# Three parts of expert tiles instead of two halves, results gathered at the join

## The chip, the cores and the metric

The kernel runs on one core of a Trainium2 chip. The metric is the device time of one execution in microseconds. The engines are TensorE (PE in the profile, PEld for its weight loads), VectorE (DVE), ScalarE (ACT), GpSimd (POOL) and SyncE (SP), which here only issues transfers.

## What is computed

One transformer layer on 2048 tokens of 128 features: attention with 16 heads and an ALiBi causal mask, then a mixture of 8 experts of which each token uses 2.

```python
h = _layernorm(x, axis=-1) * (1 + ca) + sa
x = x + ga * _L0_attn_ref(h, ...)                 # 16 heads of 8, causal, ALiBi
h = _layernorm(x, axis=-1) * (1 + cb) + sb
x = x + gb * _L0_ffn_ref(h, ...)
# _L0_ffn_ref:
logits = xf @ router_w.T
probs = jax.nn.softmax(logits, axis=-1)
top_w, top_idx = jax.lax.top_k(probs, TOPK)       # TOPK = 2
top_w = jax.nn.softmax(top_w, axis=-1)
h = jax.nn.silu(jnp.einsum('td,efd->tef', xf, w1))   # E = 8, F = 512
y = jnp.einsum('tef,edf->ted', h, w2) * expert_scale[None, :, None]
out = jnp.einsum("te,ted->td", combine, y)        # combine: the two weights of each token, else 0
```

## The kernel before, in words

Tokens lie in 16 blocks of 128, and four blocks make a chunk. Attention runs in four groups of four heads; a group has 36 steps over keys and queries (`STEPS`). In a step TensorE computes scores (L738), ScalarE exponentiates them (L1210) and TensorE multiplies by the values (L705). VectorE finds row maxima for the next group meanwhile (L966); in the last group it has none left from about step 17 on, and does other work beside the steps: the norm of each chunk's sums (L923 to L932), the residual after the projection (L608, L990), statistics, the scaled tokens (L866), and, after the transposes (L562) and the router's product (L625), the routing (`route`, L1007 to L1041).

Experts are worked on in tiles of 128 rows that belong to one expert. `count` (L633, L636) counts on TensorE how many tokens each expert gets, `place` (L1051 to L1064) turns that into a row of `slot_scratch` in DRAM for each token and choice, and an expert for each tile. This is done once for each half of the tokens, 8 blocks; a half has 16 + 7 = 23 tiles, so that every expert's rows fit. GpSimd's `send` (L1369) scatters a half's tokens, 2 x 8 indirect transfers of 128 rows. Each row also carries its weight and the row to which its result goes.

A tile then takes: SP loads the expert's w1 and the 128 rows (L517, L522); TensorE transposes the rows (L803); ScalarE scales them (L1231); TensorE multiplies by w1 (`up`, L812), ScalarE applies silu (L1237), TensorE multiplies by w2 (`down`, L822); VectorE copies w2 into place three tiles ahead (L1084) and multiplies the result by weight and gate (`keep`, L1092); GpSimd scatters it to its place in `y_scratch` (L1418). TensorE runs `up(j)` ahead of `down(j - 1)`. Every engine's program is a fixed order written out by hand; engines meet at semaphores. The first half's places are made at step 29 of the last group, the scatter follows; the second half's are made at tile 9, and GpSimd then stands its 16 scatters ahead of the results of tiles 9 and later. Between the last attention step and tile 0 come the norm, projection, residual, statistics and transposes of the last chunk. When a half's results are in DRAM, SP reads them back in order of the tokens (L530), VectorE adds them (L1098, L1099), and SP stores the output (L534).

Of the kernel before, what the change touches and what calls it, by code (L numbers as in the profile page):

```python
# [149 lines left out]
TABLES_AT, EMPTY_AT, BLANK_AT = 5, [6, 7, 8, 9], [11, 20, 25]  # L150
BIAS_AT = [28, 30, 32, 34]
NORM_AT = {12: 0, 17: 1, 21: 2}
PROJECT = {18: 0, 19: 1, 23: 2}
RESIDUAL = {18: 0, 19: 1, 24: 2}
TOKENS = {20: 0, 21: 1, 28: 2}
DOUBLE = {22: 0, 23: 1, 28: 2}
TURN = {21: 0, 22: 1, 28: 2}
LOGITS = {23: [0, 1], 30: [2]}
KEEP_LOGITS = {23: [0, 1], 30: [2]}
ROUTE = {23: 0, 24: 1, 25: 2, 26: 3, 27: 4, 28: 5}  # L160
ROUTE_EXP = {23: 0, 26: 1}
COUNT_AT = 26
PLACE_AT = 29


HALFN = NT // 2
ROW = C + 2
NTILE = HALFN * TOPK + E - 1
TILES = 2 * NTILE
DEEP = 4  # L170
FAR = 14


LATE_ROUTE = {1: 0, 3: 1, 4: 2, 5: 3, 6: 4, 8: 5}
LATE_EXP = {2: 0, 7: 1}
LATE_COUNT, LATE_PLACE = 7, 9
JOIN_AT = {NTILE + 8: 0, NTILE + 10: 1}
# [29 lines left out]
def build(nc, a):  # L207
# [3 lines left out]
    with ExitStack() as ctx:  # L211
# [90 lines left out]

        slots = sb("slots", [P, NT, TOPK, ROW])
        slots_u = slots.bitcast(mybir.dt.uint32)
# [4 lines left out]
        count_to = sb("count_to", [P, NTILE])  # L309
        more = sb("more", [P, E, E])  # L310
        tiles_of = sb("tiles_of", [P, 2, E])
        tiles_to = sb("tiles_to", [P, 2, E])
        base_at = sb("base_at", [P, E])
        passed = sb("passed", [P, NTILE, E])
        owner = sb("owner", [P, NTILE])
        expert = sb("expert", [P, 2, NTILE], mybir.dt.int32)
        spot = sb("spot", [P, 2, HALFN, E])
        spot_f = sb("spot_f", [P, 2, HALFN])
        spots = sb("spots", [P, TOPK, NT], mybir.dt.uint32)
        xt = sb("xt", [P, FAR, ROW])  # L320
        xt_u = xt.bitcast(mybir.dt.uint32)
# [5 lines left out]
        yfin = old1[:, 0:2 * TPC * TOPK * C].rearrange("p (a n k c) -> p a n k c", a=2, n=TPC, k=TOPK)  # L327
        yt = old1[:, 2 * TPC * TOPK * C:(2 * TPC * TOPK + FAR) * C].rearrange("p (k c) -> p k c", c=C)
# [8 lines left out]
        slot_dram = nc.dram_tensor("slot_scratch", (TILES * P, ROW), fp32, kind="Internal").ap()  # L337
        y_dram = nc.dram_tensor("y_scratch", (TOPK * T + TILES * P, C), fp32, kind="Internal").ap()
# [26 lines left out]
        tables_s, blank_s, blank_out = sem("tables_s"), sem("blank_s"), sem("blank_out")  # L365
        both_s, count_ps, place_s, sent_in = sem("both_s"), sem("count_ps"), sem("place_s"), sem("sent_in")
        xt_in, w1s_in = [sem(f"xt_in{k}") for k in range(FAR)], [sem(f"w1s_in{k}") for k in range(DEEP)]
        w2s_s, tT_ps, tT_s, up_ps, silu_s, down_ps, yt_s = (sem(n) for n in ("w2s_s", "tT_ps", "tT_s", "up_ps", "silu_s", "down_ps", "yt_s"))
        y_out = [sem(f"y_out{k}") for k in range(FAR)]
        y_in = [sem("y_in0"), sem("y_in1")]  # L370
# [44 lines left out]
        def tile_outs(j):  # L415

            return [(k, 16 * len(range(k, j, FAR))) for k in range(FAR) if j > k]
# [8 lines left out]
        def _(sp):  # L426
# [30 lines left out]
            def group(g, first, last):  # L457
                for p in range(-1, NSTEP):
# [10 lines left out]
                    if g == 1 and p in BLANK_AT[:2]:  # L469
                        k = BLANK_AT.index(p)  # L470
                        sp.wait_ge(blank_s, k + 1)
                        q0, q1 = (0, NT * TOPK) if k == 0 else (NT * TOPK, TILES)
                        dst = slot_dram.rearrange("(p q) c -> p (q c)", q=TILES)[:, q0 * ROW:q1 * ROW]
                        sp.dma_start(dst, slots[:, :, :, :].rearrange("p n k c -> p (n k c)")[:, 0:(q1 - q0) * ROW]).then_inc(blank_out, 16)
# [34 lines left out]
            def load_tile(j):  # L509

                k, x, half = j % DEEP, j % FAR, j // NTILE
                if j % NTILE == 0:
                    sp.wait_ge(place_s, half + 1)
                e = sp.value_load(expert[0:1, half, j % NTILE:j % NTILE + 1], min_val=0, max_val=E - 1)
                if j >= DEEP:
                    sp.wait_ge(up_ps, j - DEEP + 1)
                sp.dma_start(w1s[:, k, :], a["w1T"][:, ds(e * F, F)]).then_inc(w1s_in[k], 16)  # L517
                if j % NTILE == 0:
                    sp.wait_ge(sent_in, 16 * TOPK * HALFN * (half + 1))
                if j >= FAR:  # L520
                    sp.wait_ge(y_out[x], 16 * (j // FAR))
                sp.dma_start(xt[:, x, :], slot_dram[j * P:(j + 1) * P, :]).then_inc(xt_in[x], 16)  # L522

            def load_results(c):
                for k, n in tile_outs(NTILE * (c // 2 + 1)):
                    sp.wait_ge(y_out[k], n)
                src = y_dram[c * CW * TOPK:(c + 1) * CW * TOPK, :].rearrange("(n p k) c -> p n k c", p=P, k=TOPK)
                if c >= 2:
                    sp.wait_ge(joined, c - 1)
                sp.dma_start(yfin[:, c % 2, :, :, :], src).then_inc(y_in[c % 2], 16)  # L530

            def store_output(c):
                sp.wait_ge(joined, c + 1)
                sp.dma_start(o_v[:, c * TPC:(c + 1) * TPC, :], x_sb[:, c * TPC:(c + 1) * TPC, :]).then_inc(stored, 16)  # L534
# [311 lines left out]
        def _(dve):  # L846
# [273 lines left out]
            for c in range(2, NC_):  # L1120
                join(c)
# [354 lines left out]
```

## Time and profile before

| | |
|---|---|
| median of 3 runs | 635.05 us (630.54 to 641.14) |
| the profiled execution | 638.27 us |
| its span, first to last instruction | 636.4 us |
| TensorE busy | 506.6 us (80%) |
| VectorE busy | 442.6 us (70%) |
| ScalarE busy | 396.3 us (62%) |
| GpSimd busy | 154.8 us (24%) |
| mean granted clock of TensorE | 0.892 |

The busy shares are means over the whole span. A row of a timeline gives start, duration, engine, line, operation, tiles and count, and in brackets the idle time before it and what ended it. All times are microseconds from the start of the span. "Issue" is time in which an engine waited for nothing that the profile shows, "remote" a release by something that it doesn't show. Ends of matrix products are modelled.

### The profile page before, as it was taken

Reading aid. Unit: us, or ns where it says so; the run is one execution under the profiler, and the core shown is the slowest. Engines: PE = TensorE matmul, PEld = TensorE weight load, DVE = VectorE, ACT = ScalarE, POOL = GpSimd, SP = SyncE. Lnnn points to the kernel's source line nnn. Section 1 sums busy time; section 2 is a strip of 40 time slices with the busy share of each in tenths; the row PEclk is TensorE's granted clock in tenths of the full one; section 3 lists DMA queues with packets and bytes.
Section 4 is the critical chain, followed back from the end, with each engine's and each line's share of the span. In section 5 each row is a group of like instructions: output and inputs, shape, how many; then the busy total and the mean of one; then the engine's idle time right before and its main releaser. Section 6 shows DMA issues by size and latency. Waiting matters only on the chain.

```text
span 636.4 us, 14860 instructions
## 1 busy us (share of the span) xinstructions
PE 506.6 (80%) x5756; PEld 266.6 (42%) x5756; DVE 442.6 (70%) x677; ACT 396.3 (62%) x760; POOL 154.8 (24%) x250
## 2 busy tenths in 40 slices
PE   4657788899998999979999997979644886279991
PEld 2422232333433432423432432434212886279891
DVE  3789989899989989869989899586303264024532
ACT  4822456688887888768888887765622562035450
POOL 3410000001041114103031103051540135734451
PEclk9955899999999999979999999996857689569997
DMA  5691600000154013241000001000120244246863
GB/s 143 210 283 23 102 2 1 3 4 5 34 87 155 3 62 133 51 66 20 2 4 2 3 9 19 3 1 1 51 80 21 72 145 143 75 123 202 255 203 115
DMA packets 36627, 46.33 MB, mean 73 GB/s; under 512 B 6328, under 2 KB 27512, under 8 KB 36184
## 3 DMA queue, kind: packets, MB, share of 16 engines
q1 hardware_dynamic: 33728, 39.84, 23.5%
q0 software_dynamic: 2496, 5.15, 2.3%
q8 instruction: 46, 0.75, 0.5%
q10 hardware_dynamic: 336, 0.42, 0.2%
q14 instruction: 21, 0.17, 0.1%
HBM read 29.45 MB, written 15.74 MB: 71 GB/s over the span
## 4 chain that ended last, share of the span: by engine, by line
PE 44%; DVE 7%; issue 6%; ACT 6%; DMA 4%; another core or an unknown queue 2%; SPq 1%; POOL 1%; DVEq 0%; POOLq 0%; ACTq 0%
PE pv L705 14%; PE b L738 9%; PE b L812 6%; PE b L822 5%; ACT probs L1210 5%; PE b L677 4%; DVE part L966 2%; PE b L652 2%; DMA xt<-slot_scratch 1%; DMA y_scratch<-aug,xt 1%; DVE slots L866 1%; DMA sums_scratch<-raw 1%; ACT raw L1182 1%; PE b L803 1%
## 5 line engine op out<-in xcount | busy, mean ns | idle before, releaser
L1210 ACT ACTIVATE probs<-b 128x512 f32<-128x512 f32 (+1 forms) x576 | 298.6, 570 | 106.5 <-PE b L652 38.2
L966 DVE TENSOR_REDUCE part<-b 128x2 f32<-128x1024 f32 (+2 forms) x320 | 327.1, 1060 | 32.8 <-PE b L677 15.7
L705 PE MATMUL pv<-probs,v_cur 128*32 128x256 f32 (+1 forms) x2432 | 181.5, 380 | 2.8 <-issue 2.5
L738 PE MATMUL b<-aug 55*128 55x512 bf16 (+3 forms) x640 | 116.8, 362 | 37.4 <-ACT probs L1210 28.7
L677 PE MATMUL b<-aug 52*128 52x512 bf16 (+3 forms) x640 | 118.0, 369 | 22.3 <-DVE part L966 19.9
L738 PEld LDWEIGHTS b<-aug 55*128 55x128 bf16 x640 | 36.8, 94 | 154.2 <-ACT probs L1210 139.6
L705 PEld LDWEIGHTS pv<-probs,v_cur 128*32 128x32 f32 x2432 | 50.7, 110 | 72.4 <-issue 43.7
L812 PE MATMUL b<-hTt,aug 128*128 128x128 f32 x368 | 54.1, 295 | 11.0 <-issue 10.2
L822 PE MATMUL b<-aug,hst 128*128 128x128 f32 x368 | 53.0, 292 | 11.9 <-issue 9.9
L1092 DVE SCALAR_TENSOR_TENSOR aug<-b,xt,gate 128x128 f32<-128x128 f32 x46 | 16.1, 350 | 64.0 <-PE b L822 31.9
L1418 POOL DMA_INDIRECT y_scratch<-aug,xt x46 | 44.6, 970 | 63.0 <-DVE aug L1092 60.9
L812 PEld LDWEIGHTS b<-hTt,aug 128*128 128x128 f32 x368 | 49.9, 210 | 12.0 <-issue 12.0
L822 PEld LDWEIGHTS b<-aug,hst 128*128 128x128 f32 x368 | 49.0, 207 | 12.6 <-issue 11.7
L677 PEld LDWEIGHTS b<-aug 52*128 52x128 bf16 x640 | 34.0, 96 | 38.6 <-DVE part L966 31.5
L1237 ACT ACTIVATE hst<-b 128x512 f32<-128x512 f32 x46 | 27.5, 597 | 33.3 <-PE b L812 14.1
L1231 ACT ACTIVATE hTt<-b,modc 128x128 f32<-128x128 f32 x46 | 20.9, 456 | 36.4 <-PE b L803 23.7
L1326 POOL CAST nmp<-nmax 128x16 bf16<-128x16 f32 x16 | 3.4, 213 | 143.3 <-POOLq L183 143.1
L1369 POOL DMA_INDIRECT slot_scratch<-slots,spots x32 | 31.4, 980 | 17.1 <-issue 9.1
L652 PE MATMUL b<-maskQ,identh 64*128 64x128 bf16 (+1 forms) x512 | 34.0, 217 | 0.0
L1084 DVE COPY aug<-w2T_sb 128x512 f32 x46 | 20.0, 435 | 19.6 <-issue 19.1
L652 PEld LDWEIGHTS b<-maskQ,identh 64*128 64x128 bf16 x512 | 26.6, 102 | 13.0 <-issue 2.5
L652 PE MATMUL b<-maskT_sb,identh 64*128 64x128 bf16 (+1 forms) x512 | 30.8, 207 | 0.0
(152 smaller groups left out, 343.7 us busy)
## 6 DMA issues: line engine op xcount, KB each, us to landing
aug<-in_w1T SPq DMA_DIRECT2D x46, 256.0 KB
xt<-slot_scratch SPq DMA_DIRECT2D x46, 65.0 KB
aug<-q_scratch SPq DMA_DIRECT2D x6, 384.0 KB
aug<-k_scratch SPq DMA_DIRECT2D x6, 384.0 KB
slot_scratch<-slots SPq DMA_DIRECT2D x1, 2080.0 KB, 7.9
w2T_sb<-in_w2T SPq DMA_DIRECT2D x1, 2048.0 KB, 8.8
aug<-y_scratch SPq DMA_DIRECT2D x4, 512.0 KB
q_scratch<-pieces SPq DMA_DIRECT2D x4, 384.0 KB, 2.9
```

What stands on the lines that cost most here:

```text
L652: ins = mm(pair[half][:, at_ + c0:at_ + c1], identh[k, h, :], table[k, h, c0:c1], start=False, stop=True, skip_group_check=True)
L677: ins = mm(pair[half][:, at_:at_ + w], q_aug[buf][n, b, t:t + P], k_aug[buf][n, b, c * CW:c * CW + w], start=True, stop=True)
L705: return mm(pv[32 * hh:32 * hh + 32, c0:c1], v_cur[:, kb, hh, :], probs[:, step_ % 2, hh, at_:at_ + c1 - c0], start=(kb == 0 and c0 == 0), ...
L738: done.append(mm(pair[half][:, at_:at_ + w], k_aug[g % 2][n, b, kb * P:kb * P + P], q_aug[g % 2][n, b, (j + 1) * CW - w:(j + 1) * CW], sta ...
L812: last = mm(b1[:, j % 2, f * P:(f + 1) * P], w1s[:, k, f * P:(f + 1) * P], hTt[:, j % 2, :], start=True, stop=True)
L822: last = mm(b1[:, 2 + j % 2, 0:C], hst[:, j % 2, f, :], w2s[:, k, f, :], start=(f == 0), stop=(f == FC - 1))
L966: ins = nc.vector.tensor_reduce(dst, b1[:, slot:slot + 2, at_:at_ + w], AX.X, ALU.max)
L1210: nc.scalar.activation(probs[:, p % 2, hh, 0:w], b2[:, (n2 - 1) % RING2, 0:w], ACT.Exp).then_inc(exp_done, 1)
L1231: nc.scalar.activation(hTt[:, j % 2, :], b2[:, j % 2, 0:P], ACT.Identity, bias=modc[:, 2:3], scale=modc[:, 3:4]).then_inc(tT_s, 1)
L1237: nc.scalar.activation(hst[:, j % 2, :, :].rearrange("p f t -> p (f t)"), b1[:, j % 2, :], ACT.Silu).then_inc(silu_s, 1)
L1369: nc.gpsimd.indirect_dma_start(slot_dram, bass.IndirectOffsetOnAxis(ap=spots[:, b, n:n + 1], axis=0), slots[:, n, b, :], None).then_inc(se ...
L1418: nc.gpsimd.indirect_dma_start(y_dram, bass.IndirectOffsetOnAxis(ap=xt_u[:, k, C:C + 1], axis=0), yt[:, k, :], None).then_inc(y_out[k], 16)
```

## The change

The tokens are split in three parts of 4, 8 and 4 blocks, with 15, 23 and 15 tiles. The rows in `slot_scratch` carry the 128 features alone. A tile's result goes to `y_scratch` in tile order, by a plain store from SP six tiles later; when all tiles of a part are stored, GpSimd gathers the rows of each block, one indirect transfer for each of the two choices, and VectorE multiplies by the weight when it adds. The work on the last chunk moves from ahead of tile 0 into tiles 3 to 19. Routing in the last group is no longer placed at steps, but stands behind all of VectorE's maxima.

```diff
+PARTS = [(0, TPC), (TPC, 3 * TPC), (3 * TPC, NT)]
+NTILES = [TOPK * (n1 - n0) + E - 1 for n0, n1 in PARTS]
+LATE_PROJECT, LATE_RESIDUAL, LATE_TOKENS, LATE_TURN, LATE_LOGITS, LATE_KEEP = 3, 4, 6, 7, 9, 10
+LATE_COUNT, LATE_PLACE = 16, {17: 0, 18: 1, 19: 2}
+JOIN_AT = {27: 0, 28: 1, 29: 2, 30: 3, 44: 4, 46: 5, 48: 6, 50: 7, 52: 8}
+SEND_BREAK = 8
...
             for j in range(TILES):
                 load_tile(j)
-                if j in JOIN_AT:
-                    load_results(JOIN_AT[j])
+                if j >= STORE_BEHIND:
+                    store_tile(j - STORE_BEHIND)
...
-            pe.wait_ge(place_s, 1)
-            for i in range(TPC):
-                project(NC_ - 1, i)
-            turn_late(NC_ - 1)
+            pe.wait_ge(place_s, 2)
             turn_tile(0)
...
-                V.scalar_tensor_tensor(yt[:, k, :], b1[:, 2 + j % 2, 0:C], xt[:, k, C + 1:C + 2], gate[:, 1, :], ALU.mult, ALU.mult).then_inc(yt_s, 1)
+                V.tensor_tensor(yt[:, k, :], b1[:, 2 + j % 2, 0:C], gate[:, 1, :], ALU.mult).then_inc(yt_s, 1)
...
+            def send_part(k):
+
+                n0, n1 = PARTS[k]
+                pool.wait_ge(xn_s, NC_ + n1 // TPC)
+                pool.wait_ge(blank_out, BLANKS)
                 pool.wait_ge(place_s, k + 1)
-                own.wait()
-                for n in range(HALFN * k, HALFN * (k + 1)):
+                for n in range(n0, n1):
+                    if k == 1 and n == n0 + SEND_BREAK // TOPK:
+                        deviation(NC_ - 1)
+                    send(k, n)
+
+            def gather_part(k):
+
+                for m, n_out in tile_outs(BASE[k + 1]):
+                    pool.wait_ge(y_out[m], n_out)
+                for n in range(*PARTS[k]):
                     for b in range(TOPK):
-                        nc.gpsimd.indirect_dma_start(slot_dram, bass.IndirectOffsetOnAxis(ap=spots[:, b, n:n + 1], axis=0), slots[:, n, b, :], None).then_inc(sent_in, 16)
+                        nc.gpsimd.indirect_dma_start(yfin[:, n, b, :], None, y_dram[0:BASE[k + 1] * P, :], bass.IndirectOffsetOnAxis(ap=spots[:, b, n:n + 1], axis=0)).then_inc(y_in[n], 16)
...
+            deviation(0)
+            deviation(1)
+            deviation(2)
+            send_part(0)
+            send_part(1)
+            gather_part(0)
+            send_part(2)
+            gather_part(1)
+            gather_part(2)
```

GpSimd's program from the scatter of the first half on, before: L1259 and L1268 are the deviation of a chunk, L1348 doubles the tokens, L1369 scatters tokens, L1418 results.

```order
L1369 DMA slot_scratch<-slots,spots 5888x130 x16
L1259 TENSOR_SCALAR rstd<-mv 128x4
L1268 TENSOR_TENSOR rstd<-rstd,neg_half 128x4
L1348 COPY slots<-slots 128x4x128
L1418 DMA y_scratch<-aug,xt 9984x128 x9
L1369 DMA slot_scratch<-slots,spots 5888x130 x16
L1418 DMA y_scratch<-aug,xt 9984x128 x37
```

The same place now; L1381 scatters tokens, L1400 gathers results.

```order
L1381 DMA slot_scratch<-slots,spots 6784x128 x16
L1293 TENSOR_SCALAR rstd<-mv 128x4
L1302 TENSOR_TENSOR rstd<-rstd,neg_half 128x4
L1381 DMA slot_scratch<-slots,spots 6784x128 x8
L1400 DMA raw<-y_scratch,spots 128x128 x8
L1381 DMA slot_scratch<-slots,spots 6784x128 x8
L1400 DMA raw<-y_scratch,spots 128x128 x24
```

The first 16 are part 0's 8 and the first 8 of part 1. The 46 scatters of results are gone from this queue; 32 gathers stand behind the tokens' scatters.

TensorE's program from its last attention products into the first tiles, before:

```order
L705 MATMUL pv<-probs,v_cur 32x128 x16
L608 MATMUL pv<-wproj_sb,yn 128x128 x4
L562 MATMUL b<-ident_sb,slots 128x128 x4
L803 MATMUL b<-ident_sb,xt 128x128 x2
L812 MATMUL b<-hTt,aug 128x128 x4
L625 MATMUL pv<-rwT_sb,hT 128x8 x4
```

and now:

```order
L706 MATMUL pv<-probs,v_cur 32x128 x16
L804 MATMUL b<-ident_sb,xt 128x128 x2
L813 MATMUL b<-hTt,aug 128x128 x4
L804 MATMUL b<-ident_sb,xt 128x128
L813 MATMUL b<-hTt,aug 128x128 x4
L823 MATMUL b<-aug,hst 128x128 x4
```

The projection (L608) and the transposes (L562) of the last chunk stand behind tiles 3 and 7 now, its router product (L625) behind tile 9.

## Rows read from the trace of the kernel before

**Rows 1.** Chain of waits in order of time (start, us, what), from the attention's end.
```profile
483.12 0.61 ACT raw L1182
...
496.44 2.04 PE b L812 x8
...
624.57 2.23 DMA y_scratch<-aug,xt
626.98 3.83 DMA aug<-y_scratch
```

**Rows 2.** Timeline of TensorE, two quiet tiles and the last products.
```profile
567.02 1.06 PE L812 MATMUL b<-hTt,aug 128*128 128x128 f32 x8
...
568.91 1.06 PE L812 MATMUL b<-hTt,aug 128*128 128x128 f32 x8
...
621.59 2.03 PE L822 MATMUL b<-aug,hst 128*128 128x128 f32 x16
```

**Rows 3.** Windows: busy time of each engine in two stretches, granted clock, DMA share.
```profile
456.00:473.00 17.00, 4.19 (x30) 0.90 (x30) 1.07 (x3) 2.50 (x5) 11.14 (x12) 0.55 0.15 48
535.60:563.50 27.90, 7.86 (x38) 6.85 (x37) 2.37 (x7) 2.94 (x6) 17.35 (x19) 0.57 0.25 79
```

**Rows 4.** Timeline of GpSimd, first and last of 16 and of 21 scatters.
```profile
450.11 1.25 POOL L1369 DMA_INDIRECT slot_scratch<-slots,spots  x1 [4.97 <-DVE spots L1064]
...
469.53 0.96 POOL L1369 DMA_INDIRECT slot_scratch<-slots,spots  x1 [0.31 <-issue]
...
530.75 0.96 POOL L1369 DMA_INDIRECT slot_scratch<-slots,spots  x1 [2.97 <-DVE spots L1064]
...
556.21 0.96 POOL L1418 DMA_INDIRECT y_scratch<-aug,xt  x1 [0.30 <-issue]
```

**Rows 5.** Waits from 450 to 476: total us, times, longest.
```profile
ACT probs L1210 <- remote: 14.5, 3, 6.6
```

**Rows 6.** Timeline of TensorE and ScalarE in the first burst.
```profile
455.98 0.39 PE L738 MATMUL b<-aug 55*128 55x512 bf16 x2 [0.66 <-issue]
...
460.23 1.09 ACT L1210 ACTIVATE probs<-b 128x512 f32<-128x512 f32 x2 [3.90 <-remote]
```

**Rows 7.** Timeline of TensorE and ScalarE in the second burst.
```profile
533.84 1.06 PE L812 MATMUL b<-hTt,aug 128*128 128x128 f32 x8
...
540.92 0.60 ACT L1237 ACTIVATE hst<-b 128x512 f32<-128x512 f32 x1 [3.88 <-remote]
541.62 2.04 PE L822 MATMUL b<-aug,hst 128*128 128x128 f32 x8 [3.35 <-issue]
...
563.43 1.91 PE L812 MATMUL b<-hTt,aug 128*128 128x128 f32 x8
```

**Rows 8.** Timeline of GpSimd and VectorE in quiet tiles.
```profile
609.75 0.96 POOL L1418 DMA_INDIRECT y_scratch<-aug,xt  x1 [0.93 <-DVE aug L1092]
609.94 0.43 DVE L1084 COPY aug<-w2T_sb 128x512 f32 x1 [0.46 <-issue]
```

**Rows 9.** Timeline of VectorE, scaled tokens, start of routing, first and last of placing.
```profile
420.39 5.21 DVE L866 TENSOR_SCALAR slots<-x_sb,mv,rstd 128x128 f32<-128x128 f32 x4 [0.47 <-POOL rstd L1268]
...
437.42 0.19 DVE L1011 TENSOR_REDUCE psm<-wqkv 128x8 f32<-128x64 f32 x1
...
446.63 0.23 DVE L1051 TENSOR_TENSOR more<-b,steps 128x64 f32<-128x64 f32 x1
...
449.63 0.17 DVE L1064 CAST spots<-spot_f 128x16 uint32<-128x16 f32 x1
```

**Rows 10.** Timeline of TensorE, router product of chunk 2, first transposes of a tile.
```profile
453.37 1.06 PE L625 MATMUL b<-rwT_sb,hT 128*128 128x8 f32 x8
...
494.92 0.63 PE L803 MATMUL b<-ident_sb,xt 128*128 128x128 f32 x2
```

**Rows 11.** Timeline of the sync queue, two token loads in a row.
```profile
471.82 0.34 SPq L522 DMA_DIRECT2D xt<-slot_scratch  x1
...
473.35 0.43 SPq L522 DMA_DIRECT2D xt<-slot_scratch  x1
```

More of the change, by code:

```diff
@@ L415, in tile_outs @@
         def tile_outs(j):
-            return [(k, 16 * len(range(k, j, FAR))) for k in range(FAR) if j > k]
+            return [(k, 16 * len(range(k, j, OUT_DEEP))) for k in range(OUT_DEEP) if j > k]
         def shared(u, first):
@@ L468, in group @@
                             load_alibi(sp, g + 1, (g + 1) % 2, aug_in)
[L469 to L474, printed above, removed]
+                    if g == 1 and p == BLANK_AT:
+                        sp.wait_ge(empty_s, 1)
+                        rows_of = slot_dram.rearrange("(p q) c -> p (q c)", q=TILES)
+                        for q0 in range(0, TILES, NT):
+                            q1 = min(q0 + NT, TILES)
+                            sp.dma_start(rows_of[:, q0 * C:q1 * C], slots[:, 0:q1 - q0, :].rearrange("p n c -> p (n c)")).then_inc(blank_out, 16)
                     if g and p == SUMS_OUT:
@@ L509, in load_tile @@
             def load_tile(j):
[L511 to L514, printed above, removed]
+                k, x, part_ = j % DEEP, j % ROWS_DEEP, TILE_PART[j]
+                if j == BASE[part_]:
+                    sp.wait_ge(place_s, part_ + 1)
+                e = sp.value_load(expert[0:1, j:j + 1], min_val=0, max_val=E - 1)
                 if j >= DEEP:
@@ L536, in _ @@
             for j in range(TILES):
                 load_tile(j)
[L538 to L546 removed]
+                if j >= STORE_BEHIND:
+                    store_tile(j - STORE_BEHIND)
+                if j in STORE_AT:
+                    store_output(TPC * STORE_AT[j], TPC * (STORE_AT[j] + 1))
@@ L549, in _ @@
+            for j in range(TILES - STORE_BEHIND, TILES):
+                store_tile(j)
+            outputs = [(TPC, 2 * TPC), (2 * TPC, 3 * TPC), (3 * TPC, NT - 2), (NT - 2, NT)]
+            for n0, n1 in outputs:
+                store_output(n0, n1)
+            sp.wait_ge(stored, 16 * (len(STORE_AT) + len(outputs)))
         @block.tensor
@@ L837, in _ @@
                     down(j - 1)
-                if j == 0:
+                if j == LATE_PROJECT:
+                    for i in range(TPC):
+                        project(NC_ - 1, i)
+                if j == LATE_TURN:
+                    turn_late(NC_ - 1)
+                if j == LATE_LOGITS:
                     logits(NC_ - 1)
                 if j == LATE_COUNT:
-                    count(1)
+                    count(NPART - 1)
             down(TILES - 1)
@@ L976, in group @@
                 dve.sem_inc(s1_ready, -n_task)
-                mine.reset()
+                if not last:
+                    mine.reset()
             V = nc.vector
@@ L1066, in _, with place_part @@
+            def place_part(k):
+                for piece in range(3):
+                    place(k, piece)
             dve.wait_ge(mask_in, 6 * 16)
@@ L1119, in _ @@
             keep(TILES - 1)
-            for c in range(2, NC_):
-                join(c)
+            for n in range(len(JOIN_AT), NT):
+                join(n)
         @block.scalar
@@ L1377, in group @@
                         values(3, g)
-                    if last and p in RESIDUAL:
-                        deviation(RESIDUAL[p])
                     if g == 1:
```

342 lines of the change are left out of this document (162 added, 180 removed).

## The prediction

> **What bounds the kernel now.** I first read the chain of waits, to find which stretch sets the end. After the last attention product the chain goes through VectorE (the sums of the last chunk, its residual, its statistics), reaches the first expert product at 496.44, and then alternates between up and down products of tiles, whose last ends at 623.6; a tail of scatter, read-back and addition closes the span [rows 1, 2]. Where nothing disturbs it, a tile takes 568.91 - 567.02 = 1.89 us, and TensorE has no gap: it is the bound there [rows 2]. In two stretches, though, it is busy only 4.19 of 17 us (from 456 to 473) and 7.86 of 27.9 us (from 535.6 to 563.5) [rows 3]. These two holes are the most important thing in the profile.
>
> Then I looked at what each engine does in the holes. GpSimd issues indirect scatters back to back, one every 1.27 to 1.29 us: 16 from 450.11 to 470.5, and 21 (16 of the second half, then 5 results that had queued behind them) from 530.75 to 557.2 [rows 4]. In the first hole ScalarE waits three times, 14.5 us together, for something that the profile calls remote [rows 5], though TensorE's scores were there: the pair of 455.98 ends by 456.4 and the exponential on it starts at 460.23 [rows 6]. In the second the up product of 533.84 ends by 534.9, but the activation behind it starts at 540.92 [rows 7]. So TensorE's completions reach the others late while indirect transfers run without a pause. The other direction is not late: TensorE starts at 541.62, a tenth of a microsecond after that activation's end [rows 7]. One scatter per tile, as the quiet tiles issue it [rows 2], does no harm. The harm begins about 5 to 6 us into a burst and ends 2.5 to 3.5 us after it. I call this a hold.
>
> **Prices of a hold.** A burst of 16 cost 14.5 us in the attention [rows 5]. The second, of 21: between the up products of 533.84 and 563.43, 29.6 us, lie three tile periods where 29.6/1.89 would be 15.6, so 12.6 x 1.89 = 24 us, and the next tile runs at the low clock (eight products in 1.91 us instead of 1.06), 1.7 us more for up and down [rows 2, 7]. For a burst of 8 (10.1 us) there is no row. Below: the one signal that comes 10 us into the first burst, 460.23 - 456.4 = 3.8 us late [rows 6]. Above: until three microseconds after the burst, 6.3 us, plus 1.7 of low clock, 8.0. I take 5.5 inside the tiles and 4.7 in the attention.
>
> **The change, part by part.**
>
> *Tiles.* Before, two halves give 2 x (16 + 7) = 46 tiles. Now parts of 4, 8 and 4 blocks give 15 + 23 + 15 = 53. Seven more at 1.89: **+13.3 us** [rows 2].
>
> *Start of the tiles.* Before, project, residual, statistics and turning of the last chunk lie ahead of tile 0; now they stand in tiles 3 to 10, and the tiles wait only for the places of part 1 (`place_s` of 2). I time both conditions. Attention: it ends at 483.1. Its hold of 14.5 us shrinks to that of part 0's burst of 8, 4.7. In steps 22 and 23 TensorE also waited on VectorE, whose four scalings took 5.21 us beside GpSimd's additions [rows 9]; in the new order of GpSimd the additions come first, so I take 5 us off (bounds 0 and 7; both my estimates from that row and the two waits behind it). 483.1 - 14.5 + 4.7 - 5 = 468.3. Places of part 1: the logits of chunk 2 (at 453.37 before [rows 10]) come at about 453, 5 us earlier but behind a hold; routing and placing took from 437.42 to 449.8, 12.4 us with four scalings among them [rows 9]. Of that the placing, 446.63 to 449.8, is 3.2 us behind the count, which TensorE does after step 34, near 465.4. So places at 468.6, and the first up product 1.5 us after the first turn, as before (494.92 to 496.44 [rows 1, 10]): 470.2. **496.4 - 470.2 = -26.2 us**. What hides VectorE's routing is the last five attention steps; without that cover it costs up to 10 us.
>
> *Late work in the tiles.* Eight products, four transposes and a wait of TensorE for the scalings in tile 6 (keep, copy and 1.1 us of scaling on VectorE in front of it). The sixteen take about 1.7 us at the high clock, by the 1.06 us for eight [rows 2], the wait about 2, less 0.7 for a count of 4 blocks in place of 8 (an estimate): **+3 us**. The routing of part 2 is shorter than that of a half.
>
> *Holds in the tiles.* Removed: 24 + 1.7 = **-25.7 us**. Added on GpSimd are five bursts. Part 1's 16 scatters are split by the deviation of chunk 3, which waits for tile 4: 8 + 8, at the tiles' start and at about tile 5. When tile 14 is stored (the sync queue runs six tiles behind), 8 gathers of part 0; part 2's 8 scatters, whose places are ready at tile 19, follow. When tile 37 is stored, near tile 41, 16 gathers of part 1. **The trace has no gather.** A gather is issued by the same engine, by the same kind of instruction, on 128 rows of 512 B, so I give it the pitch of 1.27 us [rows 4]; the two bounds of the pitch are the 0.96 us of the instruction alone [rows 8] and 1.9 us, a tile's period, at which nothing would hold. Whether it also holds TensorE's signals is the open price: below nothing, above as a scatter. The quiet tiles load their weights (128 x 512 fp32) and tokens by plain transfers, four times the bytes of a scatter and more, and hold nothing [rows 2], so volume is not the cause; what is left is GpSimd's side, which gathers share. I take the upper end: 5.5 + 5.5 (scatters) + 5.5 (gathers) + 5.5 (scatters) + 16 (16 gathers) = **+38 us**. With harmless gathers it is 16.5.
>
> *Queues.* The result's store moves from GpSimd to the sync queue, which issued two transfers per tile at a pitch of 473.35 - 471.82 = 1.53 us [rows 11]. A third transfer of 0.43 us and its wait make about 2.0 us, a little over the 1.89 of TensorE. It can lead by 4 tiles, and every hold refills the lead, so I cost it at nothing; without holds it is up to 53 x 0.12 = 6 us. VectorE's keep loses one factor and six joins move into the tiles, in its slack.
>
> *Tail.* Before, from 623.6 to 636.4: 12.8 us, of which a scatter lands 626.98 - 624.57 = 2.4 us after its start, and read-back, two pairs of additions and the store follow [rows 1]. Now: keep 0.4, store issued and landed 2.4, eight gathers 8 x 1.27 = 10.1, landing of the last 2.41 - 0.96 = 1.5, additions 0.6, store 2.4 (the three other than the gathers' by the scatter's 2.4 and the size of the additions): 17.4. **+4.6 us**.
>
> Sum: 636.4 - 26.2 + 13.3 + 3 - 25.7 + 38 + 4.6 = 643.4 of span. The profiled execution took 638.27 us, 1.87 over its span and 3.22 over the median of 635.05; so in terms of the median 643.4 + 1.87 - 3.22 = **642 us**.
>
> **A rule weighed.** Each of the 24 gathers in the tiles lies beside VectorE's fp32 copies of w2. The indirect transfer at 609.75 took 0.96 us with such a copy at 609.94 inside it [rows 8], and the last one of the attention, with no copy beside it, took 0.96 too [rows 4]. So the row says that a copy costs an indirect transfer nothing, and the sum stays. The Trainium skill, *SBUF — State Buffer*, section "SBUF: two separate sides", warns of the contrary: descriptors of a transfer from GpSimd cannot be written while VectorE runs an fp32 copy in its two-port mode. By the 620 and 3100 ns that the same page gives, gathers beside copies would take five times as long, and the run would end far later. This trace does not agree.
>
> **The rivals.**
>
> *Gathers hold nothing.* For it: only scatters are seen to hold; they write DRAM in 512 B rows, gathers read it. Against it: what is late is a signal of TensorE, not a transfer. 642 - 5.5 - 16 = **620 us**. Chance 0.27.
>
> *Bursts of 8 hold nothing either.* The first missing signal arrived 10.1 us into a burst [rows 4, 6], about as long as eight last. Then 620 - 3 x 5.5 - 4.7 = **599**, or 615 if the 16 gathers still hold. Chance 0.07.
>
> *Slower.* Place: GpSimd's queue at tile 17 to 20. If the place of part 2 is ready when the gathers of part 0 end, gathers and scatters are one burst of 16: 16 instead of 11 us. That decides alone: 647, and with the sync queue at 2.0 us per tile, or routing not covered, 650 to 655. The point is whether tile 19 is passed within 10 us of the store of tile 14; held, it is not, and half held it is. Chance 0.19. The copies' rule above: over 655, chance 0.02.
>
> **How the numbers follow.** Forecast 642, own range 634 to 650, chance 0.45. A measurement of this kernel tells about 2% from no change, 12.7 us: under 622.4 is faster, over 647.7 slower. Faster: most of the 620 case (0.22) and the short bursts (0.07), 0.29. Slower: the slower rival with the page's rule, 0.21, and 0.05 of the forecast, 0.26. The rest, 0.45, is within 2%. The range takes in part of the 615 case and all up to 655: 614 to 655.
>
> **What would show it.** Right: first up product near 470; completions of TensorE missing in all of GpSimd's bursts, gathers too; 1.89 us per tile between them; 17 us from the last product to the end. Wrong: no idle TensorE beside the gathers after tile 41 (then 620); attention's end not before 475; gathers with another pitch than 1.27 us, which the tail multiplies by eight; sync issues every 2 us with TensorE waiting for `xt`.

## The result and the profile after

The changed kernel takes 649.86 us (median of 4 runs, 648.15 to 651.03) beside 634.73 us of the kernel before (median of 4 runs, 630.54 to 641.14): ratio 1.0259, interval 1.0202 to 1.0316. The ratio is taken from the means and leaves out the slowest run of the kernel before, 641.14 us. The changed kernel is slower by 2.6%. The forecast said 642 and no change that can be measured; the time lies in its range, the verdict beyond it.

The profiled execution took 648.15 us. The first lines of its page:

```profile
span 646.3 us, 15334 instructions
...
PE 516.0 (80%) x5876; PEld 276.5 (43%) x5876; DVE 449.8 (70%) x756; ACT 402.6 (62%) x776; POOL 136.1 (21%) x230
```

GpSimd is busy 18.7 us less than before, and that shortens nothing. TensorE's timeline shows the end of attention and the start of the tiles (L706 values, L804 a tile's transposes, L813 up):

```profile
463.41 0.65 PE L706 MATMUL pv<-probs,v_cur 128*32 128x128 f32 x16 [0.17 <-ACT probs L1243]
464.95 0.41 PE L804 MATMUL b<-ident_sb,xt 128*128 128x128 f32 x2 [0.89 <-DVE spots L1071]
465.89 1.13 PE L813 MATMUL b<-hTt,aug 128*128 128x128 f32 x8 [0.53 <-ACT hTt L1264]
```

The first up product starts at 465.89, before at 496.44 [rows 1]: 30.6 us earlier. The loss lies behind it. GpSimd's timeline, first and last of the 8 gathers of part 0 (L1400) and of the 8 scatters of part 2 (L1381), then of the 16 gathers of part 1:

```profile
522.01 1.01 POOL L1400 DMA_INDIRECT raw<-y_scratch,spots  x1 [23.38 <-DMA y_scratch<-aug]
...
530.99 0.95 POOL L1400 DMA_INDIRECT raw<-y_scratch,spots  x1 [0.30 <-issue]
532.24 1.00 POOL L1381 DMA_INDIRECT slot_scratch<-slots,spots  x1 [0.30 <-issue]
...
541.13 0.96 POOL L1381 DMA_INDIRECT slot_scratch<-slots,spots  x1 [0.30 <-issue]
...
588.89 0.97 POOL L1400 DMA_INDIRECT raw<-y_scratch,spots  x1 [46.81 <-DMA y_scratch<-aug]
...
607.67 0.94 POOL L1400 DMA_INDIRECT raw<-y_scratch,spots  x1 [0.30 <-issue]
```

Gathers and scatters follow each other with 0.30 us between, one every 1.25 to 1.28 us on average. They are two runs of 16. Beside the first one, the timeline of TensorE (L823 is down) and ScalarE (L1270 is silu) has the same holes as before [rows 7]:

```profile
534.84 2.05 PE L813 MATMUL b<-hTt,aug 128*128 128x128 f32 x8 [5.10 <-issue]
...
542.80 0.60 ACT L1270 ACTIVATE hst<-b 128x512 f32<-128x512 f32 x1 [8.06 <-remote]
543.50 2.05 PE L823 MATMUL b<-aug,hst 128*128 128x128 f32 x8 [6.61 <-issue]
```

The up product of 534.84 ends by 536.9, and silu on it starts at 542.80. The windows (stretch and its length; busy us and count of PE, PEld, DVE, ACT, POOL; granted clock, DMA share, GB/s) put these holes beside the rest, as [rows 3] did:

```profile
465.00:486.00 21.00, 15.74 (x109) 14.99 (x110) 8.78 (x26) 7.98 (x15) 7.94 (x8) 0.84 0.37 113
490.00:503.00 13.00, 8.54 (x65) 8.21 (x66) 1.96 (x6) 3.50 (x7) 6.71 (x7) 0.87 0.45 131
525.20:548.50 23.30, 9.31 (x54) 8.47 (x53) 3.71 (x18) 3.54 (x7) 12.92 (x14) 0.63 0.36 105
548.50:590.40 41.90, 39.24 (x328) 36.80 (x327) 16.73 (x48) 20.08 (x39) 1.20 (x2) 1.00 0.62 182
590.40:616.00 25.60, 11.58 (x69) 10.40 (x68) 3.50 (x9) 3.95 (x8) 13.95 (x15) 0.67 0.41 113
```

TensorE has its gaps in exactly the four stretches in which GpSimd issues indirect transfers, small ones beside the first 8 and large ones beside the runs of 16. In the fourth line, where it issues two, TensorE is nearly full, but not quite: it waits for tokens. The sync queue's timeline there (L519 w1, L524 tokens, L529 store of a result), and TensorE's waits from 548 to 590 (total us, times, longest):

```profile
564.59 0.35 SPq L519 DMA_DIRECT2D aug<-in_w1T  x1
564.98 0.43 SPq L524 DMA_DIRECT2D xt<-slot_scratch  x1
565.46 0.43 SPq L529 DMA_DIRECT2D y_scratch<-aug  x1
566.63 0.35 SPq L519 DMA_DIRECT2D aug<-in_w1T  x1
```

```profile
PE b L804 <- DMA xt<-slot_scratch: 2.4, 8, 0.8
```

Two transfers took 1.53 us per tile [rows 11]; three take 566.63 - 564.59 = 2.04 us, more than TensorE's 1.89, and now and then an issue takes longer:

```profile
550.24 1.73 SPq L524 DMA_DIRECT2D xt<-slot_scratch  x1
```

The chain of waits, a load of tokens and the end:

```profile
560.10 3.22 DMA xt<-slot_scratch
...
626.38 1.88 PE b L823 x16
628.60 1.53 DMA y_scratch<-aug
...
639.86 2.47 DMA raw<-y_scratch,spots
```

From the last product (628.2) to the end of the span are 18.1 us, before 12.8 [rows 1].

**The ledger of the tiles.** It goes by the starts of the up products. Four of them bound the two long stretches of loss and the quiet one between them:

```profile
525.17 1.06 PE L813 MATMUL b<-hTt,aug 128*128 128x128 f32 x8
...
548.46 1.06 PE L813 MATMUL b<-hTt,aug 128*128 128x128 f32 x8
...
592.52 1.06 PE L813 MATMUL b<-hTt,aug 128*128 128x128 f32 x8
...
615.95 1.06 PE L813 MATMUL b<-hTt,aug 128*128 128x128 f32 x8
```

From 465.89 to 628.24 are 162.4 us. 53 tiles at 1.89 us are 100.2. The excess over 1.89 us per tile is: tiles 0 to 5, 17.66 - 9.45 less 1.7 for the projection = 6.5 (part 1's first 8 scatters); tiles 9 to 12, 14.13 - 5.67 less 0.9 for the router's product = 7.6 (its second 8); tiles 21 to 24, from 525.2 to 548.5, 23.3 - 5.67 = 17.6 (8 gathers and 8 scatters); tiles 44 to 47, from 592.52 to 615.95, 23.43 - 5.67 = 17.8 (16 gathers). Together 49.5. Tiles 24 to 44 take 44.1 where 37.8 would do: 6.3, the sync queue. What is left, 6.4, is the late work on chunk 3 (the 1.7 and 0.9 just taken off among it) and small waits.

### The profile page after: what moved, and what is told of

Same layout as the page of the kernel before. It is cut to its first block, busy times and chain, and to the rows that moved or that the text cites. A ratio compares the mean times of both kernels' runs of the same rounds, so it can differ in the third digit from the quotient of the medians.

```text
span 646.3 us, 15334 instructions
## 1 busy us (share of the span) xinstructions
PE 516.0 (80%) x5876; PEld 276.5 (43%) x5876; DVE 449.8 (70%) x756; ACT 402.6 (62%) x776; POOL 136.1 (21%) x230
## 4 chain that ended last, share of the span: by engine, by line
PE 54%; issue 9%; ACT 7%; DVE 5%; DMA 3%; SPq 1%; POOL 1%; another core or an unknown queue 1%; ACTq 0%; POOLq 0%; DVEq 0%
PE pv L706 17%; PE b L739 12%; PE b L823 7%; PE b L813 6%; PE b L678 6%; ACT probs L1243 6%; DVE part L966 3%; PE b L653 3%; DMA xt<-slot_scratch 2%; PE b L804 1%; ACT raw L1215 1%; POOL raw L1400 1%; PE b L608 1%; PE b L625 1%
## 5 line engine op out<-in xcount | busy, mean ns | idle before, releaser
L966 DVE TENSOR_REDUCE part<-b 128x2 f32<-128x1024 f32 (+2 forms) x320 | 327.0, 1061 | 29.4 <-PE b L678 14.3
L706 PE MATMUL pv<-probs,v_cur 128*32 128x256 f32 (+1 forms) x2432 | 179.0, 376 | 3.1 <-issue 2.7
L739 PE MATMUL b<-aug 55*128 55x512 bf16 (+3 forms) x640 | 115.2, 358 | 28.3 <-ACT probs L1243 24.1
L739 PEld LDWEIGHTS b<-aug 55*128 55x128 bf16 x640 | 36.7, 93 | 141.8 <-ACT probs L1243 134.2
L706 PEld LDWEIGHTS pv<-probs,v_cur 128*32 128x32 f32 x2432 | 50.4, 109 | 71.2 <-issue 44.6
L823 PE MATMUL b<-aug,hst 128*128 128x128 f32 x424 | 61.8, 293 | 22.3 <-issue 21.9
L813 PE MATMUL b<-hTt,aug 128*128 128x128 f32 x424 | 61.5, 292 | 15.1 <-issue 14.6
L1103 DVE TENSOR_TENSOR aug<-b,gate 128x128 f32<-128x128 f32 x53 | 15.4, 290 | 82.0 <-remote 46.0
L823 PEld LDWEIGHTS b<-aug,hst 128*128 128x128 f32 x424 | 56.8, 208 | 23.7 <-issue 23.6
L813 PEld LDWEIGHTS b<-hTt,aug 128*128 128x128 f32 x424 | 55.9, 205 | 16.6 <-issue 16.6
L1270 ACT ACTIVATE hst<-b 128x512 f32<-128x512 f32 x53 | 31.6, 596 | 47.3 <-remote 26.4
L1264 ACT ACTIVATE hTt<-b,modc 128x128 f32<-128x128 f32 x53 | 24.1, 456 | 51.3 <-PE b L804 33.2
L1400 POOL DMA_INDIRECT raw<-y_scratch,spots x32 | 30.5, 953 | 101.5 <-DMA y_scratch<-aug 92.7
L1095 DVE COPY aug<-w2T_sb 128x512 f32 x53 | 23.1, 436 | 24.0 <-issue 22.9
L1381 POOL DMA_INDIRECT slot_scratch<-slots,spots x32 | 31.4, 982 | 31.0 <-DVE spots L1071 22.2
```

Source lines behind the costliest of these rows:

```text
L706: return mm(pv[32 * hh:32 * hh + 32, c0:c1], v_cur[:, kb, hh, :], probs[:, step_ % 2, hh, at_:at_ + c1 - c0], start=(kb == 0 and c0 == 0), ...
L739: done.append(mm(pair[half][:, at_:at_ + w], k_aug[g % 2][n, b, kb * P:kb * P + P], q_aug[g % 2][n, b, (j + 1) * CW - w:(j + 1) * CW], sta ...
L813: last = mm(b1[:, j % 2, f * P:(f + 1) * P], w1s[:, k, f * P:(f + 1) * P], hTt[:, j % 2, :], start=True, stop=True)
L823: last = mm(b1[:, 2 + j % 2, 0:C], hst[:, j % 2, f, :], w2s[:, k, f, :], start=(f == 0), stop=(f == FC - 1))
L966: ins = nc.vector.tensor_reduce(dst, b1[:, slot:slot + 2, at_:at_ + w], AX.X, ALU.max)
L1264: nc.scalar.activation(hTt[:, j % 2, :], b2[:, j % 2, 0:P], ACT.Identity, bias=modc[:, 2:3], scale=modc[:, 3:4]).then_inc(tT_s, 1)
```

## The experiments

Twelve kernels were run beside the two; all but the last start from the changed one. Most of them use one tool, a pause of GpSimd behind an indirect transfer: a small memset on a scratch tile of its own, waited for. It moves no data of the kernel and takes no transfer away; it changes only how closely they follow. The last 8 gathers, behind the last tile, keep their pace. Six kernels were executed once, and a single total says little: in executions with the same code up to there, and no pause, the first up product starts at 464.6, 465.9, 465.9, 468.3, 472.1 and 475.2 us (pace_gather, the change, plain_gather, act_store, no_gather, plain_long). So the six are judged by the stretch beside the transfers.

```diff
+            def pause(w):
+
+                own.inc(nc.gpsimd.memset(acc[:, 0:w], 0.0))
+                own.wait()
...
                     nc.gpsimd.indirect_dma_start(slot_dram, ..., slots[:, n, :], None).then_inc(sent_in[k], 16)
+                    pause(512)
...
                         nc.gpsimd.indirect_dma_start(yfin[:, n, b, :], None, ...).then_inc(y_in[n], 16)
+                        if k < NPART - 1:
+                            pause(512)
```

> Behind every indirect transfer of GpSimd except the last part's eight gathers stands a memset of 128 x 512 fp32 (about 0.5 us) that GpSimd waits for, so the pitch goes from 1.27 to about 1.85 us; nothing else changes. Theory (the holds come from transfers that follow without a pause): at that pitch, that of the quiet tiles of the kernel before, the idle TensorE of the four bursts in the tiles is gone (about 6 + 7 + 17 + 17 us beyond 1.89 us per tile), the gathers of part 1 take 30 us in place of 20 but end before the tiles do, and the time falls from 650 to 600-610 us. Rival (the holds come from the number of indirect transfers, or from the DRAM traffic that they start, whatever their pitch): the holds only last longer, 645-665 us.

Measured: 608.74 us (607.0 to 612.26), ratio 0.9554 to the kernel before (0.951 to 0.9597), span 607.6. GpSimd's timeline in part 1's gathers, the window over all 16, and the page's group of `keep`:

```profile
563.40 0.98 POOL L1406 DMA_INDIRECT raw<-y_scratch,spots  x1 [22.07 <-DMA y_scratch<-aug]
564.38 0.54 POOL L1380 MEMSET acc<- 128x512 f32 x1
565.19 0.97 POOL L1406 DMA_INDIRECT raw<-y_scratch,spots  x1 [0.27 <-POOL acc L1380]
```

```profile
563.40:592.00 28.60, 22.87 (x187) 20.98 (x185) 13.07 (x34) 10.69 (x20) 24.51 (x32) 0.98 0.62 172
```

```profile
L1103 DVE TENSOR_TENSOR aug<-b,gate 128x128 f32<-128x128 f32 x53 | 15.4, 290 | 40.0 <-PE b L823 27.9
```

The same group of the changed kernel was

```profile
L1103 DVE TENSOR_TENSOR aug<-b,gate 128x128 f32<-128x128 f32 x53 | 15.4, 290 | 82.0 <-remote 46.0
```

At 1.79 us from the first transfer to the second, and 1.81 in the mean, with the same transfers and more work on GpSimd, `keep` no longer waits for anything "remote", and no stretch of TensorE is empty: 22.87 of 28.6 us where it was 11.58 of 25.6. So the loss is the close succession of the transfers, not the transfers. What is left over is the sync queue: 2.26 us per tile in the mean from tile 22 on, and once, about tile 14, tokens that arrive late because the queue waits for the paced scatters of part 1, the last of which is issued at 494.03 (it loads these tokens at 496.73, L524):

```profile
498.63 0.48 PE L804 MATMUL b<-ident_sb,xt 128*128 128x128 f32 x1 [2.71 <-DMA xt<-slot_scratch]
```

**How long the pause must be.** Three runs change it: 256 columns, 64 columns, and four memsets of 512 behind every fourth transfer (`n % 2 and b`) with none between.

```diff
-                    pause(512)
+                    pause(256)
```

> As the paced kernel, with half the memset (128 x 256): a pitch near 1.55 us in place of 1.8. If what counts is a rest of any length between two indirect transfers, no hold: 603-610 us. If what counts is their rate, the hold comes back in part, later in a burst than at 1.27 us: 615-640 us.

> The changed kernel with a pause of one 64-column memset behind each indirect transfer, so a pitch of about 1.4 us. If the pitch has to leave the transfer's own issue some tenths of a microsecond of free time, this is already enough and the span is as with 256 columns, 605 to 610 us. If the price falls in proportion to the pitch between 1.26 us (about 32 us of holds in the tiles) and 1.56 us (none), about half of them stay: some 625 us.

> The changed kernel with four memsets of 512 columns (about 2.5 us) behind every fourth indirect transfer and none between, so runs of four at a pitch of 1.26 us, the mean pitch about 1.9 us. If a hold needs more than some 5 us of unbroken transfers (idle time of TensorE began 5 to 6 us behind the first of a burst), there is none here: span 605 to 612 us. If every transfer without a pause adds its share (about 1 us each, 8 us per 8), three quarters of the price stay: some 630 us.

Measured, one execution each: 256 columns 609.36 us (span 607.6), 64 columns 634.24 (span 632.4), every fourth 613.24 (span 611.4). The windows over part 1's 16 gathers, in this order:

```profile
564.90:592.00 27.10, 22.20 (x187) 20.87 (x185) 11.73 (x36) 10.69 (x20) 21.57 (x32) 1.00 0.65 182
```

```profile
577.50:603.00 25.50, 16.28 (x94) 14.46 (x92) 4.82 (x14) 5.76 (x11) 18.15 (x32) 0.69 0.48 133
```

```profile
564.90:592.00 27.10, 22.71 (x181) 20.59 (x180) 9.59 (x26) 10.04 (x20) 22.06 (x29) 1.00 0.59 166
```

With 256 columns the transfers follow every 1.54 to 1.74 us, 1.62 in the mean of these 16, and hold nothing. At 1.41 us (64 columns) TensorE issues 94 products there instead of 187; the excess of its tiles is 4.2, 3.7, 15.0 and 15.2 us at the four places, 38.1 beside 49.5 at 1.26. The fourth counts from tile 44 to 48, the third from 22 to 26. So the price does not fall in proportion to the pitch, as one theory of that run had it, and is not gone, as the other had it: over three quarters remain at 1.41, nothing at 1.62. A memset between two transfers is therefore not enough by itself; the pitch decides. Runs of four at full pace with a rest of some 2.7 us are nearly harmless. From 560 to 592 three signals still come late to ScalarE, by 2.5 us at most, and TensorE loses 2.8 us to three waits:

```profile
ACT hTt L1264 <- remote: 3.3, 2, 2.4
...
ACT hst L1270 <- remote: 2.5, 1, 2.5
```

A run of four lasts 5 us, so this agrees with the start of a hold some 5 us into a run, as it was read from the trace of before [rows 4, 6].

**Which transfers do it.** The pause behind the 24 gathers alone (the cut is against the kernel with 512 columns behind gathers and scatters):

```diff
                     nc.gpsimd.indirect_dma_start(slot_dram, ..., slots[:, n, :], None).then_inc(sent_in[k], 16)
-                    pause(512)
```

> The changed kernel with the 512-column pause behind the 24 gathers of parts 0 and 1 alone; all scatters run at 1.26 us as before. The gathers' holds should go (about 17.8 us at the 16 of part 1, and 9 to 10 of the 17.6 us where 8 gathers stood ahead of 8 scatters), those of three bursts of scatters in the tiles stay (6.5 + 7.6 + 7 to 8 us): span 620 to 624 us. If gathers are the whole matter, it comes to the 608 us of the version with all pauses; if scatters are, it stays over 635 us.

Measured: 624.3 us (620.94 to 627.3), ratio 0.981 (0.9761 to 0.9858), span 619.1. The excess beside the gathers is gone: tiles 44 to 47, from 578.4 to 585.4, take 7.0 us where they took 23.5, the sync queue's share in it. Those of the scatters stay; TensorE beside part 2's, which run from 533.88 to 544:

```profile
540.75 0.27 PE L804 MATMUL b<-ident_sb,xt 128*128 128x128 f32 x1
544.62 2.05 PE L813 MATMUL b<-hTt,aug 128*128 128x128 f32 x8 [3.59 <-issue]
```

So gathers hold as scatters do, and are worth 646.3 - 619.1 = 27 us of span by the two profiled executions, each the fastest of its four.

The gathers left out; the joins of parts 0 and 1 add what lies there:

```diff
-            gather_part(0)
             send_part(2)
-            gather_part(1)
```

> The gathers of parts 0 and 1 are left out, and their joins add whatever lies there. Theory (24 gathers hold TensorE, 17 us at part 1 and about 10 of the 17.6 at part 0 with part 2's scatters): 620-626 us, with the eight scatters of part 2 alone costing 6-8 us. Rival (gathers hold nothing, the gaps beside them have another cause): 645-650 us and the same two gaps.

Measured: 628.63 us (one execution), span 626.8, some 3 us above what was expected; the tiles start at 472.1, 6 us later than in the change. No gap at tiles 44 to 47. Part 2's 8 scatters alone still hold, 14.3 us for three tiles, 8.7 over:

```profile
541.17 2.05 PE L813 MATMUL b<-hTt,aug 128*128 128x128 f32 x8 [2.29 <-issue]
```

Beside the 17.6 us of the change it separates the burst of 16 into its halves: 8.7 for the scatters alone, 8.9 more when 8 gathers stand directly ahead.

**Is it GpSimd's queue, or the indirect form?** The 24 gathers as plain transfers of the same size, also from GpSimd (the rows read are then not the right ones), and once more in two halves each, so that the stream lasts as long:

```diff
-                        nc.gpsimd.indirect_dma_start(yfin[:, n, b, :], None, ...).then_inc(y_in[n], 16)
+                        if k < NPART - 1:
+                            nc.gpsimd.dma_start(yfin[:, n, b, :], y_dram[n * P:(n + 1) * P, :]).then_inc(y_in[n], 16)
+                        else:
+                            nc.gpsimd.indirect_dma_start(yfin[:, n, b, :], None, ...).then_inc(y_in[n], 16)
```

> The 24 gathers of parts 0 and 1 are plain transfers of 128 rows, still issued by GpSimd and still without a pause, so their rows are not the wanted ones. Theory A (it is the descriptors that GpSimd generates, indirect or not): the holds at the gathers stay, 635-650 us. Theory B (it is the indirect addressing): no hold at the gathers of part 1, and only part 2's eight scatters hold in front of them, 620-628 us.

> The 24 gathers of parts 0 and 1 are plain transfers of GpSimd again, each now in two halves of 64 columns, so that part 1's burst is 32 transfers and 18 us long, as long as that of the gathers; their rows are not the wanted ones. If the indirect form is what holds TensorE: no hold beside them, 620-628 us. If any unbroken stream from GpSimd holds it once it is longer than the 9 us of the earlier plain kernel: about 10-15 us of idle TensorE in part 1, 632-645 us.

Measured, one execution each: 622.93 us (span 621.1) and 634.41 (span 632.6; its tiles start only at 475.2, and more of them run at the sync queue's pace). GpSimd's rows at part 1, of the one and of the other, and all waits of TensorE from 587 to 606 in the second:

```profile
578.91 8.89 POOL L1401 DMA_DIRECT2D raw<-y_scratch  x16 [42.24 <-DMA y_scratch<-aug]
```

```profile
587.49 18.26 POOL L1402 DMA_DIRECT2D raw<-y_scratch  x32 [37.32 <-DMA y_scratch<-aug]
```

```profile
PE b L804 <- DMA xt<-slot_scratch: 1.8, 4, 0.7
```

32 plain transfers in 18.26 us, one every 0.57 us and without a pause, delay no signal; beside them TensorE waits for tokens alone, 1.8 us together. In both runs the 8 scatters of part 2, issued right behind the plain ones, hold as ever (8.0 us in the first). So it is the indirect form. The total of the second lies in the range that was expected if any unbroken stream holds, 632 to 645 us; the stretch beside the transfers shows that this isn't why, since nothing is held there, and the tiles had started 9.3 us later than in the change.

**The sync queue.** The stores of results from ScalarE, three tiles behind, in place of the sync queue:

```diff
-                sp.wait_ge(yt_s, j + 1)
-                sp.dma_start(y_dram[j * P:(j + 1) * P, :], ...)
+                act.wait_ge(yt_s, j + 1)
+                act.dma_start(y_dram[j * P:(j + 1) * P, :], ...)
```

> The stores of the tiles' results are issued by ScalarE, behind the silu of the tile three later, in place of the sync queue. Theory (between the holds the sync queue is the bound, with three issues per tile): tiles 28 to 44 fall from 2.2 to 1.9 us each, 6 us less: 642-645 us. Rival (the tiles of that stretch wait for the latency of the token rows or for traffic): the same 2.2 us per tile and 649-651 us. Holds of about 50 us stay in both.

Measured: 647.08 us (644.64 to 648.75), ratio 1.0136 (1.0103 to 1.0169), span 647.0. The windows over the quiet tiles and over part 1's gathers:

```profile
548.00:589.00 41.00, 40.23 (x337) 39.96 (x338) 18.88 (x59) 21.73 (x42) 0.00 (x0) 0.93 0.69 198
589.40:614.00 24.60, 9.79 (x66) 8.99 (x65) 3.48 (x10) 4.00 (x8) 15.33 (x16) 0.67 0.36 100
```

Tiles 25 to 44 now take 1.92 us each, and of the 6.3 us 1.0 is left from tile 24 to 44: the rest was the sync queue. The median lies above the 642 to 645 us expected of this cause and below the 649 to 651 of the rival. The profiled execution is the slowest of the four: its tiles start 2.4 us later and its two long holds are 1 and 2 us longer. By the ratios the version is 1.2% below the change, 7.8 us (the two intervals allow 2 to 13), about what the term is worth; the holds remain. That matches what the Trainium skill, *Trainium Kernel Development and Optimization*, section "Key Constraints", says of issuing from several engines, that it saves only the sequencer's issue time: what bound here is three issues of 0.35 to 0.43 us and the queue's own time between them, 2.04 us together.

**Both.** Pause and ScalarE's stores together, with 512 columns and then with 256:

> Both repairs: a pause of a 128 x 512 memset behind every indirect transfer except the last eight gathers, and the stores of results on ScalarE's queue. Theory (holds and sync queue were two separate losses of the changed kernel): the 2.2 to 2.3 us tiles of the paced kernel fall to 1.9 us where nothing else waits, but the 16 gathers of part 1 take 28 us and may end after the tiles: 594-604 us, 5 to 14 us under the paced kernel's 608.7. Rival (at full tile rate the paced transfers hold again, since they then share the clock with more traffic): 605-615 us.

> The changed kernel with a pause of one 256-column memset behind each indirect transfer (pitch 1.56 us) and with the stores of results issued by ScalarE. If a pitch of 1.56 us is enough and the gathers of part 1 now end before the last tile's last product, the tail shrinks by what they ran over (about 5 to 6 us of the 22 us in the version with 512 columns): span 593 to 597 us. If the joins of the tail are held by the last 8 gathers alone, there is no gain: 599 us. If the pause is too short once tiles take 1.9 us each, holds come back and it is over 605 us.

Measured: 602.15 us (600.46 to 604.28), ratio 0.9471 (0.942 to 0.9522), span 598.7; and 597.14 us (591.89 to 600.8), ratio 0.9319 (0.9256 to 0.9383), span 596.3. The second is the fastest of all, by its ratio 6.8% below the kernel before; beside the change's ratio that is 9% less. Its window over part 1's gathers, its last products, and the last piece of its chain of waits from a transfer (L814 is down here):

```profile
555.40:576.00 20.60, 20.40 (x180) 20.03 (x179) 9.97 (x29) 10.05 (x20) 17.28 (x26) 1.00 0.73 207
```

```profile
574.13 2.03 PE L814 MATMUL b<-aug,hst 128*128 128x128 f32 x16
```

```profile
589.78 2.55 DMA raw<-y_scratch,spots
```

TensorE is busy 20.40 of 20.6 us beside the gathers, which follow every 1.59 us in the mean of the 16. The tail is 596.3 - 576.2 = 20.1 us, still longer than the change's 18.1, because part 1's gathers run until 580 and the last 8 stand behind them. The span of 596.3 lies in the expected 593 to 597 us, and the reason given there is right in kind: the shorter pause lets the gathers end sooner. It gave less than expected, though. With 512 columns the tail is 598.7 - 576.0 = 22.7 us, so it shrank by 2.6 us, not by 5 to 6.

**The attention of the kernel before.** The pause of 512 columns behind each of the first half's 16 scatters, in the kernel before:

```diff
                         nc.gpsimd.indirect_dma_start(slot_dram, ..., slots[:, n, b, :], None).then_inc(sent_in, 16)
+                        if k == 0:
+                            pause(512)
```

> The kernel before, with the pause of a 128 x 512 memset behind each of the first half's 16 scatters, which run beside the last attention steps. Theory (the three late exponentials, 14.5 us, are a hold by that burst): they go, the attention ends near 469, and since the burst is 9 us longer but ends by 479, 620-626 us against 637. Rival (the attention waits there for something else, as the load of w1 or of instructions): 634-640 us.

Measured: 625.87 us (623.28 to 627.69), ratio 0.9821 (0.9764 to 0.9878), span 625.1. The first up product comes at 484.65 instead of 496.44 [rows 1]. ScalarE's waits for scores from 450 to 476, which were 14.5 us of "remote" [rows 5], are now

```profile
ACT probs L1210 <- PE b L652: 1.4, 5, 0.4
...
ACT probs L1210 <- PE b L738: 0.9, 1, 0.9
```

This is the same hold in another kernel and beside another kind of work, and it goes by the same means: the tiles start 11.8 us sooner, of the 14.5. The hold among the tiles, whose burst has no pause, stays (15.6 and 9.2 us for two tiles).

## Why the prediction was right and wrong

**Right: what bounds the kernel, and the mechanism.** The prediction read two holes as signals of TensorE that come late beside unbroken indirect transfers of GpSimd, and put a price on each burst of the new order. The pauses show the cause in three ways: the loss goes when the transfers stand further apart, for gathers as for scatters, in both kernels. Its argument that "what is left is GpSimd's side, which gathers share" gave the right answer, but plain transfers from the same queue hold nothing; what the gathers share is the indirect form. The pitch of a gather, taken as 1.27 us, is 1.25 in part 1. The rule in the Trainium skill, *SBUF — State Buffer*, section "SBUF: two separate sides", that GpSimd can't write a transfer's descriptors beside certain fp32 copies of VectorE, is again not borne out: in the fastest version 16 gathers take 0.95 to 1.08 us each while VectorE is busy 9.97 of 20.6 us, its copies of w2 among it.

**Right: the tail.** 17.4 us forecast, 18.1 measured.

**Too cautious: the start.** Forecast 470.2, measured 465.9, so -30.6 in place of -26.2. The hold in the attention is about as forecast: TensorE's longest wait there is 4.80 us, by its timeline (L739 scores), and 4.7 were taken:

```profile
446.50 0.61 PE L739 MATMUL b<-aug 55*128 55x512 bf16 x2 [4.80 <-ACT probs L1243]
```

The last product of attention starts at 463.4 where 468.3 was forecast for its end. What saved the rest was not tried, and it may be nothing of the change: in the five other executions without a pause that have the same code up to there, it starts at 462.2, 463.5, 465.8, 469.6 and 472.7. An error of 4.3 us is within that scatter.

**Mis-sized: the holds, 38 against 49.5.** Of the terms that lay too low it is the largest. The bursts of 8 cost 6.5 and 7.6 (5.5 forecast), the 16 gathers 17.8 (16 forecast). The largest part is the step "8 gathers of part 0; part 2's 8 scatters ... follow", counted as 5.5 + 5.5: they are one run of 16 with 0.30 us between, and cost 17.6. The prediction named this as the deciding point of its *Slower* rival (tile 19 passed within 10 us of the store of tile 14) and gave it 5 us and a chance of 0.19. It happened: the gathers began at 522.01, beside tile 20, and the places of part 2 were ready at 525.9, before the last of them.

**Wrong: the sync queue at nothing.** The text has the 2.0 us per tile (measured 2.04) and the possible 6 us (measured 6.3), and then sets the term to nothing since "every hold refills the lead". The lead is not four tiles of time: w1 of tile j is issued once up(j - 4) is done, the tokens stand behind it in the same queue, and their 3.2 us until they land count too. The three periods from the start of up(j - 4) to the transposes of tile j are 5.7 us; less 1.1 for the up product itself, 0.4 for the issue of w1 and 3.2 for the tokens, about 1 us is left, an estimate from these rows. And the queue itself is released late by a hold, since it waits for TensorE's signals as well. At 2.04 us with a slow issue here and there, that is gone after four tiles (the first late start is tile 28); the trace shows eight waits there. The prediction had named sync issues every 2 us with TensorE waiting for `xt` as a sign of being wrong. (How the lead is spent is read from the rows, and was not tried by itself; that the queue is the cause was, by the stores on ScalarE.)

**Wrong, and hidden: the base of the sum.** The sum took the whole span of before and changed parts of it. In before the tiles took 127.2 us; 46 at 1.89 are 86.9, and the removed holds 25.7; the remaining 14.6 us (low clock at the start of the tiles, the count among them, small waits) were carried over unnamed. They did not come back: in the ledger above nothing beyond the 6.4 us of late work is left over. The low clock is the plainest case: before, TensorE stood idle ahead of tile 0 and its first eight up products took 2.04 us [rows 1]; now they take 1.13. Added up: -4.3 at the start, +11.5 holds, +6.3 sync queue, +3.4 late work, +0.7 tail, -14.6 carried over make +3.0, and 643.4 became 646.3 (rounded). The closeness of the forecast is therefore partly luck: errors of 22 us and 19 us against each other.

The outcome is that of the *Slower* rival as it was described, gathers and scatters in one burst and the sync queue at 2.0 us, only that the total of 649.9 came out a little under its 650 to 655. The rivals with harmless gathers or harmless bursts of 8 are excluded by the runs above.

**What stays open.** Why TensorE's signals are late. The trace names the releaser only "remote", and no run here examined GpSimd from inside. That it is the signal and not the last product itself that comes late is read from ends that the profile models; only the starts of the products are recorded. Shown is only that it needs indirect transfers in close succession: runs of 8 and more at a mean of 1.41 us or less hold, at 1.59 us or more they don't, and runs of four cost little. Where between 1.41 and 1.59 us it ends was not tried.

## What to carry to other kernels

Look for stretches in which every engine waits and one queue of GpSimd is busy: a pause between indirect transfers, which lengthens each by some 0.35 us, gave back 38.7 us of span here (646.3 to 607.6). When a change moves work, build the new stretch up from its own items (tiles x period, bursts, queue) and not only as differences to the old one, or losses that were never named are carried along. And when a term is "nothing, because something else hides it", look how many periods the cover lasts.

## What the runs showed that had not been expected

- 0.2 us of pitch decide: 1.41 us per indirect transfer keeps 38.1 of 49.5 us of holds, 1.59 to 1.62 us none.
- The form of the transfer decides, not its queue or volume: 32 plain transfers from GpSimd at 0.57 us delay no signal, 8 indirect ones at 1.26 us cost 6.5 to 8.7 us.
- A burst of 16 costs 17.6 to 17.8 us, as two of 8 and a little more, for 8 gathers and 8 scatters as for 16 gathers.
